# Recommender tower on one core: lookups in three places of a unit, the last block's layers per tile of 128

## The reference

```python
e = stack([tbl_f[ids[:, f]] for f in range(27)], axis=1)     # 2048 x 27 x 128, fp32
dot = einsum('bnd,bmd->bnm', e, e)                           # all pairs of a sample's features
z = dot.reshape(2048, 27 * 27)[:, pairs i < j]               # 351 columns
h = concatenate([z, dense_ctx], axis=1)                      # 367 columns
h = maximum(h @ W_top1 + b_top1, 0)                          # 512
h = maximum(h @ W_top2 + b_top2, 0)                          # 256
y = h @ W_top3                                               # 2048 x 1
```

## Time and profile before

| | us |
|---|---|
| runs | 377.6, 379.4, 384.47 |
| median | 379.4 |
| profiled execution | 376.98 |
| its span, first to last instruction | 375.2 |
| mean granted clock of TensorE | 0.973 |

### The profile page before, as it was taken

One profiled execution on the slowest core, in us unless ns is written; L12 is line 12 of the kernel. 1 busy time (PEld: TensorE's weight loads), 2 busy tenths in 40 slices (PEclk: granted clock), 3 DMA queues, 4 the chain that ended last, 5 costly groups with the idle time before them and its releaser, 6 DMA issues.

```text
span 375.2 us, 14179 instructions
## 1 busy us (share of the span) xinstructions
PE 331.5 (88%) x6216; PEld 302.7 (81%) x6216; DVE 250.1 (67%) x757; ACT 134.3 (36%) x235; POOL 252.3 (67%) x271
## 2 busy tenths in 40 slices
PE   0776679788799999999999999999899999996786
PEld 0665679678699988998999988998799988995775
DVE  3899577697477669765876769666776769622031
ACT  2353424532222533333333343333233343344122
POOL 5777777777777777777777777777777777760000
PEclk9999698999899999999999999999999999999699
DMA  7999954248644665348544754447634755354410
GB/s 171 239 214 231 225 142 100 81 94 190 115 91 96 141 146 113 84 90 193 127 80 101 162 131 105 93 107 178 112 87 94 163 125 113 79 120 90 79 41 1
DMA packets 59215, 46.39 MB, mean 124 GB/s; under 512 B 38499, under 2 KB 53186, under 8 KB 59153
## 3 DMA queue, kind: packets, MB, share of 16 engines
q1 hardware_dynamic: 50705, 28.16, 35.0%
q0 software_dynamic: 8448, 17.32, 19.6%
HBM read 38.37 MB, written 7.09 MB: 121 GB/s over the span
## 4 chain that ended last, share of the span: by engine, by line
PE 62%; DMA 12%; POOL 11%; DVE 8%; issue 6%; ACT 1%; POOLq 0%
PE onehot_ps L593 16%; PE onehot_ps L595 13%; POOL rows L353 11%; PE dots_ps L621 10%; DMA idb<-ids_onehot 8%; DVE mask L494 7%; PE tile_ps L605 6%; PE mlp_ps L627 5%; PE mlp_ps L629 5%; PE mlp_ps L628 5%; DMA rows<-tbl,idx 3%; PE mlp_ps L662 2%; DMA idx<-ids_gather 1%; DVE z_lo L532 0%; DVE z_hi L529 0%
## 5 line engine op out<-in xcount | busy, mean ns | idle before, releaser
L353 POOL DMA_INDIRECT rows<-tbl,idx x264 | 251.5, 953 | 82.5 <-issue 79.6
L494 DVE TENSOR_SCALAR mask<-idb,cmp 125x256 fp32r<-125x256 int32 x672 | 208.8, 381 | 54.1 <-PE onehot_ps L595 32.2
L593 PE MATMUL onehot_ps<-mask,tab_hi 125*128 125x256 f32 x672 | 175.9, 300 | 28.5 <-DVE mask L494 17.6
L595 PE MATMUL onehot_ps<-mask,tab_lo 125*128 125x256 f32 x672 | 166.3, 284 | 0.0
L593 PEld LDWEIGHTS onehot_ps<-mask,tab_hi 125*128 125x128 f32 x672 | 129.6, 193 | 35.7 <-DVE mask L494 17.1
L595 PEld LDWEIGHTS onehot_ps<-mask,tab_lo 125*128 125x128 f32 x672 | 130.3, 194 | 0.0
L621 PEld LDWEIGHTS dots_ps<-emb 128*27 128x27 f32 x4096 | 45.4, 106 | 19.6 <-issue 16.4
L377 ACT COPY emb<-tile_ps 128x512 f32<-128x512 f32 x66 | 44.1, 671 | 46.9 <-PE tile_ps L605 45.4
L621 PE MATMUL dots_ps<-emb 128*27 128x27 f32 x4096 | 54.8, 194 | 6.3 <-issue 5.6
L368 ACT COPY emb<-onehot_ps 128x512 f32<-128x512 f32 (+1 forms) x46 | 36.3, 789 | 57.3 <-PE onehot_ps L595 54.7
L605 PE MATMUL tile_ps<-ident,rows 128*128 128x128 f32 x264 | 40.9, 279 | 4.5 <-DMA rows<-tbl,idx 4.5
(11 more groups left out here) (30 smaller groups left out, 153.0 us busy)
## 6 DMA issues: line engine op xcount, KB each, us to landing
idb<-ids_onehot SPq DMA_DIRECT2D x84, 128.0 KB
dots_dram<-dots SPq DMA_DIRECT2D x28, 216.0 KB
emb<-tbl SPq DMA_DIRECT2D x11, 448.0 KB
rows<-tbl,idx POOLq DMA_INDIRECT x264
zT<-dots_dram SPq DMA_DIRECT2D x14, 117.0 KB
dots_dram<-dots SPq DMA_DIRECT2D x8, 108.0 KB, 2.9
zT<-dots_dram SPq DMA_DIRECT2D x7, 104.0 KB
emb<-tbl SPq DMA_DIRECT2D x11, 52.0 KB
```

Of the source, the lines that this page charges most:

```text
L353: nc.gpsimd.indirect_dma_start(rows[:, n % RING, i, :], None, tables[feature][:, :], bass.IndirectOffsetOnAxis(idx[:, at:at + 1], 0)).then ...
L494: made = nc.vector.tensor_scalar(mask[0:VP, n % MASK_RING, c, :], idb[0:VP, k % IDB_RING, :], cmp[0:VP, at:at + 1], None, ALU.is_equal)
L593: nc.tensor.matmul(out, tab_hi[0:VP, f, at, :], mask[0:VP, k % MASK_RING, c, :], start=(at == 0), stop=False)
L595: done = nc.tensor.matmul(out, tab_lo[0:VP, f, at, :], mask[0:VP, k % MASK_RING, c, :], start=False, stop=(at == CHUNKS - 1))
```

## The change

- In a unit, TensorE does the first two parts before the dots, the next two after them, then the unit's layer work, then the rest (`BEFORE_DOTS`, `BEFORE_LAYERS`). ScalarE's copies follow the same order; VectorE's order stays.
- Layer 1 of block 6 stands behind unit 2 of block 7 (`LAYERS_AT`), ahead of unit 3.
- The layers of block 7 are done per tile of 128 samples, with 128 moving columns: split, layer 1, relu, split of h1, layer 2, relu, layer 3, copy, and a store of y for each tile. Both tiles stand behind layers 2 and 3 of block 6.
- Of the four stores of the last tile's dots SP issues two and ScalarE two. SP loads z of tile 0 before its stores of tile 1; before, it was after them.
- The number of features in a group and the loads of ids are written in a more general form.

```diff
 UNIT_Q = 8
 PARTS_UNTIL = [6, 12, 18, 24, 29, 34, 39, NO * PARTS]
+BEFORE_DOTS, BEFORE_LAYERS = 2, 4
 SPLIT_Z_AT, LAYER1_AT, SPLIT_H1_AT, LAYER2_AT, LAYER3_AT = 3, (3, 4, 5, 6), (5, 7), 7, 0
+LAYERS_AT = 2
 GROUPS_AT = {0: [0], 1: [1], 2: [2], 3: [3, 4]}
 FIRST_GROUPS_AT = {1: 0, 2: 1, 3: 2, 5: 3, 6: 4}
+def pair_ends(f, h):
+    return h == PARTS - 1 and (f % 2 == 1 or f == NO - 1)
 def unit_parts(u):
...
                              dense[:, b * BLK:(b + 1) * BLK].rearrange("(c p) x -> p c x", c=2)
                              ).then_inc(dense_in, 16)
-            def store_dots(b, at, src, ng, landed):
-                for s in range(QUAD):
-                    dst = bass.AP(dots_dram.tensor, b * P * FEATURES * NQ + at + s * ng,
-                                  [[FEATURES * QUAD * ng, PAD], [QUAD * ng, FEATURES], [1, ng]])
-                    sp.dma_start(dst, src[PAD * s:PAD * (s + 1), :].rearrange("p (j g) -> p j g", g=ng)
-                                 ).then_inc(landed, 16)
+            def store_dots(b, at, src, ng, landed, samples_of_quad=range(QUAD)):
+                for s in samples_of_quad:
+                    sp.dma_start(*dots_store(b, at, src, ng, s)).then_inc(landed, 16)
             def load_z(b, at, cols, ng, arrived):
...
             half = FEATURES * NQ // TILES
             for q in range(TILES):
                 sp.wait_ge(dots_ps_empty, UNITS * LAST + UNITS_TILE * (q + 1))
                 store_dots(LAST, q * P * half, dots[:, LAST % 2, q * half:(q + 1) * half], NQ // TILES,
-                           last_out[q])
-            load_dense(LAST)
-            for q in range(TILES):
+                           last_out[q], range(QUAD) if q == 0 else range(QUAD // 2))
+                if q == 0:
+                    load_dense(LAST)
                 sp.wait_ge(last_out[q], 16 * QUAD)
                 load_z(LAST, q * P * half, slice(q * P, (q + 1) * P), NQ // TILES,
                        z_in if q == 0 else last_z_in)
             store_y(LAST - 1)
+            for q in range(TILES):
+                sp.wait_ge(mlp_ps_empty, MLP_FREED * (LAST + q + 1))
+                sp.dma_start(y[0:1, LAST * BLK + q * P:LAST * BLK + (q + 1) * P],
+                             y_sb[:, q * P:(q + 1) * P]).then_inc(y_last_out, 16)
             sp.wait_ge(y_out, 16 * LAST)
-            store_y(LAST)
-            sp.wait_ge(y_out, 16 * BLOCKS)
+            sp.wait_ge(y_last_out, 16 * TILES)
...
             def empty_y(b):
                 act.wait_ge(mlp_ps_full, MLP_STEPS * (b + 1))
-                if b < LAST:
-                    dst = y_sb.rearrange("p (g s) -> p g s", s=QUAD)
-                    src = mlp_ps[0:1, 0, 0:BLK].rearrange("p (s g) -> p g s", s=QUAD)
-                else:
-                    dst = y_sb.rearrange("p (q g s) -> p q g s", q=TILES, s=QUAD)
-                    src = mlp_ps[0:1, 0, 0:BLK].rearrange("p (q s g) -> p q g s", q=TILES, s=QUAD)
-                nc.scalar.copy(dst, src).then_inc(mlp_ps_empty, 1)
+                nc.scalar.copy(y_sb.rearrange("p (g s) -> p g s", s=QUAD),
+                               mlp_ps[0:1, 0, 0:BLK].rearrange("p (s g) -> p g s", s=QUAD)
+                               ).then_inc(mlp_ps_empty, 1)
...
+            def relu1_tile(q):
+                act.wait_ge(mlp_ps_full, MLP_STEPS * (LAST + q) + M1)
+                nc.scalar.activation(h1_hi[:, :, q * P:(q + 1) * P],
+                                     mlp_ps[:, q, :].rearrange("p (m b) -> p m b", m=M1),
+                                     ACT.Relu).then_inc(h1_hi_ready, 1)
+            def relu2_tile(q):
+                if q == 0:
+                    act.wait_ge(y_out, 16 * LAST)
+                act.wait_ge(mlp_ps_full, MLP_STEPS * (LAST + q) + M1 + M2)
+                for m in range(M2):
+                    nc.scalar.activation(h2[:, m, q * P:(q + 1) * P], mlp_ps[:, q, m * P:(m + 1) * P], ACT.Relu,
+                                         bias=b2_sb[:, m:m + 1]).then_inc(mlp_ps_empty, 1)
+            def empty_y_tile(q):
+                act.wait_ge(mlp_ps_full, MLP_STEPS * (LAST + q + 1))
+                nc.scalar.copy(y_sb[:, q * P:(q + 1) * P].rearrange("p (g s) -> p g s", s=QUAD),
+                               mlp_ps[0:1, q, M2 * P:(M2 + 1) * P].rearrange("p (s g) -> p g s", s=QUAD)
+                               ).then_inc(mlp_ps_empty, 1)
             def split_w1_hi():
...
                                 act.wait_ge(lo_ready, NO)
                             empty_group(t, g)
+                    parts = unit_parts(u) if b < LAST else []
+                    for f, h in parts[:BEFORE_DOTS]:
+                        if pair_ends(f, h):
+                            empty_onehot(b + 1, f // 2)
                     empty_dots(b, u)
-                    if b < LAST:
-                        for f, h in unit_parts(u):
-                            if h == PARTS - 1 and (f % 2 == 1 or f == NO - 1):
-                                if b == 0 and f == 1:
-                                    act.wait_ge(lo_ready, NO)
-                                empty_onehot(b + 1, f // 2)
+                    for f, h in parts[BEFORE_DOTS:BEFORE_LAYERS]:
+                        if pair_ends(f, h):
+                            empty_onehot(b + 1, f // 2)
                     if b == 0 and u == 4:
                         split_w1_hi()
                     if b == 0 and u == 5:
                                 relu1(b - 1, k)
                         if u == LAYER2_AT:
                             relu2(b - 1)
-            for b in (LAST - 1, LAST):
-                for k in range(M1 // 2):
-                    relu1(b, k)
-                relu2(b)
-                empty_y(b)
+                    for f, h in parts[BEFORE_LAYERS:]:
+                        if pair_ends(f, h):
+                            empty_onehot(b + 1, f // 2)
+                    if b == LAST and u == LAYERS_AT:
+                        for k in range(M1 // 2):
+                            relu1(b - 1, k)
+            act.wait_ge(dots_ps_empty, UNITS * BLOCKS)
+            for s in range(QUAD // 2, QUAD):
+                nc.scalar.dma_start(*dots_store(LAST, P * LAST_HALF, dots[:, LAST % 2, LAST_HALF:2 * LAST_HALF],
+                                                NQ // TILES, s)).then_inc(last_out[1], 16)
+            relu2(LAST - 1)
+            empty_y(LAST - 1)
+            for q in range(TILES):
+                relu1_tile(q)
+                relu2_tile(q)
+                empty_y_tile(q)
...
+            def split_z_tile(q, c):
+                if q == 0:
+                    if c == 0:
+                        dve.wait_ge(dense_in, 16 * BLOCKS)
+                    dve.wait_ge(z_in[c], (32 if c == 2 else 16) * BLOCKS)
+                else:
+                    dve.wait_ge(last_z_in[c], 32 if c == 2 else 16)
+                k, cols = K_ROWS[c], slice(q * P, (q + 1) * P)
+                nc.vector.tensor_copy(z_hi[0:k, c, cols], zT[0:k, c, cols]).then_inc(z_hi_ready, 1)
+                dve.wait_ge(z_hi_ready, 3 * (LAST + q) + c + 1)
+                nc.vector.tensor_tensor(z_lo[0:k, c, cols], zT[0:k, c, cols], z_hi[0:k, c, cols].bitcast(f32),
+                                        ALU.subtract).then_inc(z_split, 1)
+            def split_h1_tile(q):
+                dve.wait_ge(h1_hi_ready, M1 // 2 * LAST + q + 1)
+                cols = slice(q * P, (q + 1) * P)
+                nc.vector.scalar_tensor_tensor(h1_lo[:, :, cols], mlp_ps[:, q, :].rearrange("p (m b) -> p m b", m=M1),
+                                               0.0, h1_hi[:, :, cols].bitcast(f32), ALU.max, ALU.subtract
+                                               ).then_inc(h1_split, 1)
...
-            for b in (LAST - 1, LAST):
+            for c in range(3):
+                split_z(LAST - 1, c)
+            for k in range(M1 // 2):
+                split_h1(LAST - 1, k)
+            for q in range(TILES):
                 for c in range(3):
-                    split_z(b, c)
-                for k in range(M1 // 2):
-                    split_h1(b, k)
+                    split_z_tile(q, c)
+                split_h1_tile(q)
         @block.tensor
...
                                             start=(c == 0), stop=(c == M2 - 1))
                 done.then_inc(mlp_ps_full, 1)
+            def layers_tile(q):
+                cols = slice(q * P, (q + 1) * P)
+                pe.wait_ge(mlp_ps_empty, MLP_FREED * LAST)
+                for m in range(M1):
+                    for c in range(3):
+                        if m == 0:
+                            pe.wait_ge(z_split, 3 * (LAST + q) + c + 1)
+                        k, rows_of = K_ROWS[c], slice(m * P, (m + 1) * P)
+                        done = product(mlp_ps[:, q, m * P:(m + 1) * P], w1_hi[0:k, c, rows_of], w1_lo[0:k, c, rows_of],
+                                       z_hi[0:k, c, cols], z_lo[0:k, c, cols], c == 0, c == 2)
+                    done.then_inc(mlp_ps_full, 1)
```

(57 more changed lines are left out.)

13 lines of the change are left out of this document (9 added, 4 removed).

## The result

The changed kernel takes 400.92 us (median of 4 runs, 397.5 to 401.9), the kernel before, beside it, 380.23 us (4 runs). The ratio is 1.060, with a 95% interval of 1.055 to 1.065. Every ratio here leaves out the runs that took over 1.5% more than the fastest of the same kernel, every median keeps them (the two medians alone would give 1.054). The prediction said 390.0 us, slower: the sign was right and 401 lies in the range, but the added time, forecast 10.6 us, was half of what came. The profiled execution took 401.3 us with a span of 399.5 us, 24.3 us more than the span of before; those 24.3 are to be found.

What follows compares the result with a forecast made beforehand. No single engine bounds the kernel, but GpSimd's gathers set a floor of 40.0 us a block. +3.1 - 0.5 + 8.0 = +10.6 on 376.98 gives 387.6; the median lies 2.4 higher: 390.0, range 380 to 408.

Steps and rivals of the forecast that it cites:

- Block 0, forecast +3.1: Block 0: weight conversions and masks behind later dots, stores 2.75 us later, plus 0.35 in unit 3 of block 1.
- the forecast of the stores: Block 0: the stores of its dots, starting at 82.03 in the kernel before, slip by 2.75 us.
- the 0.35 that the prediction adds behind them: Unit 3 of block 1: layer 1 stands ahead of two lookup parts and needs the z split, ending 0.35 us later.
- Blocks 2 to 6, forecast -0.5: Blocks 2 to 6: stores start 0.47 us earlier, unit 3 ends 0.35 later; net -0.1 a block, -0.5 for five.
- Rival 4: Units 2 and 3: bursts of 6 parts starve for masks, bursts of 2 do not; 5.7 us won, chance 0.08.
- Schedule up to tile 0: Block 7: layer 1 of block 6 waits for z, unit 3's dots and stores follow later, tile 0 starts at 363.9.
- The added wait: Behind unit 2 of block 7: TensorE idle for most of 4.6 us, waiting for z of block 6.
- A tile, forecast 8.4 us: Block 7's layers: 60 products of 128 columns at 0.09 us plus 3.0 us not overlapped; the tail +8.0 us.
- the two ends of 0.06 and 0.24: Pace of a 128-column product: 0.06 us is half of 256 columns' 0.118; 0.24 is layer 3's plain fp32.
- Rival 2: Block 7's tiles: 128-column products cost 0.21 to 0.24 us like plain fp32; 405 to 408 us, chance 0.16.
- Rival 3: Delays covered: block 0's absorbed, clock up through the z wait, products at 0.06; 381, half covered 384; chance 0.24.
- the -1 for layer 2: Rival 3's term for layer 2 of block 6: 1 us less if the clock stays up through the z wait.

Runs made afterwards that it cites:

- the pair of runs: Kernel before with only the lookups in three places, old tail: 382.8 us, ratio 1.010; the same with block 0 in the old order: 378.7 us, ratio 1.002.
- the run from block 1 on: Kernel before with only the lookups in three places, from block 1 on, block 0 in the old order: 378.7 us, ratio 1.002.
- the tiles of 256 columns: Changed kernel, each product of the two tiles streaming its 128 columns twice, half the result unused: 393.2 us, ratio 1.039.
- halving alone: Kernel before, each product of block 7's layers 1 and 2 done as two of 128 columns: 389.2 us, ratio 1.024.
- the tiles alone: Kernel before with only block 7's layers per tile of 128, SP's new order and the two store queues: 397.3 us, ratio 1.051.

## Why the prediction was half right

**Block 0, forecast +3.1: right, the size in part by luck.** Unit 3 of block 1 ends at 110.16 instead of 107.07, +3.1. The mechanism is shown by the pair of runs: without the new order in block 0 the cost is gone. But the forecast of the stores was low (+2.75, measured 85.98 against 82.03, +3.95). With the 0.35 that the prediction adds behind them, unit 3 would have ended 4.3 later; why only 3.1 arrived there stays open.

**Blocks 2 to 6, forecast -0.5: not seen.** The lag grows from 3.1 at block 1 to 3.4 at the end of unit 7 of block 6 (340.28 against 336.91). The difference of under 1 us is less than I can explain; the run from block 1 on shows no effect of the order there, and cannot tell -0.5 from 0. Rival 4, starving bursts of masks, is refuted by the same run: it would have given 5.7 us back.

**Schedule up to tile 0: right.** The prediction's times, moved by 3.1 - 0.5, against the trace: z of block 6 whole 349.2, measured 349.7; first store of tile 0 356.2, measured 356.3; one code wait of over 2 us left, 2.73; z of tile 0 366.2, measured 367.3; tile 0 starts 366.5, measured 366.1. The added wait was shorter than said, because part of it went into the arrival of the first two z pieces, and the result was the same. For block 6's layer 2 the prediction added 0.6 to 1 us at the lower clock; its products ran 0.118 apart. The clock stayed at 1.00 across the code wait of 2.73 us, where the kernel before had lost it behind waits of 2.46 and 2.58.

**A tile, forecast 8.4 us: the step that failed.** The prediction took "0.09, between the two nearest rows: 5.4 + 3.0 = 8.4 a tile". Measured were 14.7 and 16.5. Together that is 31.2 against 16.8, +14.4, and with 0.4 for the earlier start and 0.3 for the shorter end it makes up the whole 13.7 by which the span (399.5 against 385.8) missed. Two things are in it. First, at full clock the products ran 0.111 apart, not 0.09, and what nothing overlaps was 3.3, as the tiles of 256 columns show (10.3 less 60 x 0.117). That makes 60 x 0.111 + 3.3 = 10.0 a tile, and 3.2 of the 14.4. Second, the clock: 31.2 - 20.0 = 11.2 us, at 0.213 a product (36 of tile 1's layer 1 in 7.7 us) from 369.5 on. Rows of products of 128 columns were not there to read, but the two ends of 0.06 and 0.24 stood in the text, and the number taken was near the optimistic end. The fall of the clock under such products stood nowhere in the sum: I had treated the clock only as something that gaps pull down.

Against the kernel before, whose last layers took 9.6, the 21.6 us more are about 6.2 for the second set of 60 products at full clock (13.3 against 7.1), 4.1 for the gaps that two chains have (6.6 against 2.5), and 11.2 for the clock.

**Rival 2 came nearer to the pace, for another reason.** It gave 405 to 408 for products at 0.21 to 0.24, and 0.21 is what came in the end, though not from the start: hence 401. But it said that products of 128 columns cost that by themselves; at full clock they cost 0.11. The pace is the clock's, and an engine that was busy for 1.83 to 2.00 of 2.00 us in the windows shown was still granted half of it.

**The cited figures had the direction right and the size wrong.** By the figures of the Trainium skill (TensorE: Matmul & The Clock Gate, Back-to-back issue gap), about 81 ns at 128 columns and 131 at 512, the time does not fall in step with the columns. The trace agrees, and more strongly: 0.111 us at 128 columns, not about 81 ns, against 0.118 at 256. The measurement decides here. The Trainium skill (TensorE: Matmul & The Clock Gate, LDWEIGHTS) puts a weight load at its columns divided by 1.2, by which, an estimate, it is 107 ns for the 128 weight columns of both forms. That is near the 0.111 us at full clock and half of the 0.213 at half clock. That the weight load sets the pace is only argued, since no run here changed the weight columns.

**Rival 3 failed on the cover.** Block 0's delay was not absorbed, and the products were not at 0.06. Its sum was also loose: with the -1 for layer 2 its terms leave +1.4, not +1.8, and half of the cover gives about 385.5, not 384.

## What to carry to other kernels

Price a tile by its instructions, not by its columns: where a stream of weight load and product runs at 0.12 us with 256 columns, half the columns cost the same, so cutting the last block in two doubles TensorE's work there and must buy more overlap than that (here 8 us, where the last layers went from 9.6 to 31.2, over half of it by the clock). When a step has no row in the trace, measure it in a small variant of the kernel, or take the pessimistic end where the whole case hangs on it. Before moving work ahead of a block's last stores, look at what it waits for: each engine behind it inherits the wait.

## What the runs showed of the chip that I had not expected

- Products of 128 columns were followed by a granted clock of 0.50 to the end of the span in the profiles of the three kernels that have them. In the kernel after and in halving alone no gap between them was over 0.38 us before the fall; in the tiles alone it came behind one of 1.41. With 256 columns and the same gaps the tiles kept 1.00, and the mean clock of that kernel's four runs was 0.969 to 0.978 against 0.937 to 0.953 for the kernel after. Why the chip does this stays open.
- The time between product starts does not depend on 128 or 256 columns at either level: 0.111 and 0.118 us at 2.4 GHz, 0.213 for both at 1.2.
- A wait of one length has no one effect: the clock stood at 1.00 behind an idle stretch of 2.73 us in the kernel after, and fell behind stretches of 2.46 and 2.58 in the kernel before.
- More columns through TensorE made a kernel 8 us faster (400.9 to 393.2) by keeping its clock.
